# Sparse FFN with routing: every task at a place of its own, sort steps on other operands and engines, DB of two tiles, convolution of three chunks on TensorE

## What is computed

```python
h = _layernorm(x) * (1 + ca) + sa
x = x + ga * _L0_attn_ref(h, ...)      # a state space block
h = _layernorm(x) * (1 + cb) + sb
x = x + gb * _L0_ffn_ref(h, ...)       # a routed FFN
```

## Time and profile before

| | us |
|---|---|
| median of 3 runs | 1594.65 (1587.15 to 1599.17) |
| profiled execution | 1594.51, of which the span is 1592.8 |
| VectorE busy | 1128.7 (71%) |
| TensorE busy | 1211.0 (76%), mean granted clock 0.859 |
| GpSimd busy | 1027.0 (64%) |
| ScalarE busy | 931.1 (58%) |

### The profile page before, as it was taken

How to read it: one execution, slowest core, us unless ns; L and a number is a source line. 1 busy time by engine, 2 the same in 40 slices (tenths; PEclk the granted TensorE clock), 3 DMA queues, 4 the chain that set the end, 5 groups by cost and what they waited for, 6 DMA issues and landing times. The chain is left out here.

```text
span 1592.8 us, 20071 instructions
## 1 busy us (share of the span) xinstructions
PE 1211.0 (76%) x5756; PEld 829.7 (52%) x5756; DVE 1128.7 (71%) x1489; ACT 931.1 (58%) x1772; POOL 1027.0 (64%) x936
## 2 busy tenths in 40 slices
PE   8887677565689898753578898744489999989892
PEld 4566454344456565542356565543356656646461
DVE  5898999998776977885488987995468688601000
ACT  5757775792677567842379667932377647333231
POOL 1676886886775657688895657688874356744222
PEclk9998677586698999966589999966799999999997
DMA  5359635313332322245543233245532335565442
GB/s 189 108 165 281 206 112 170 120 55 114 114 102 78 120 82 99 80 114 175 133 125 100 98 104 100 79 123 181 145 103 80 102 107 160 161 194 143 139 120 72
DMA packets 118929, 201.17 MB, mean 126 GB/s; under 512 B 25876, under 2 KB 34068, under 8 KB 117800
## 3 DMA queue, kind: packets, MB, share of 16 engines
q1 hardware_dynamic: 106536, 166.20, 33.4%
q0 software_dynamic: 12288, 33.69, 8.1%
HBM read 121.97 MB, written 77.88 MB: 125 GB/s over the span
## 5 line engine op out<-in xcount | busy, mean ns | idle before, releaser
L914 POOL TENSOR_TENSOR DB<-DU,BR 128x512 f32<-128x512 f32 x448 | 578.4, 1305 | 174.6 <-DVE H L1351 153.4
L1668 PE MATMUL pb<-ID,H 128*128 128x128 f32 x2048 | 360.2, 313 | 184.6 <-DVE ACC L1376 146.9
L1134 ACT ACTIVATE pb<-DELP,AN 128x512 f32<-128x512 f32 x448 | 306.2, 685 | 273.1 <-DVE H L1351 270.9
L1376 DVE SCALAR_TENSOR_TENSOR ACC<-pb,CTM,ACC 128x512 f32<-128x512 f32 x512 | 373.3, 729 | 105.2 <-PE pb L1668 104.3
L1668 PEld LDWEIGHTS pb<-ID,H 128*128 128x128 f32 x2048 | 278.0, 161 | 279.8 <-DVE ACC L1376 103.1
L1351 DVE TENSOR_TENSOR_SCAN H<-pb,DB 128x512 f32<-128x512 f32 x256 | 310.0, 1211 | 97.6 <-POOL DB L914 78.7
L1351 DVE TENSOR_TENSOR_SCAN H<-pb,ST,DB 128x512 f32<-128x512 f32 x192 | 244.2, 1272 | 14.7 <-ACT pb L1134 14.1
L1221 ACT ACTIVATE YO<-pb,SCO 128x512 f32<-128x512 f32 x106 | 72.3, 682 | 164.4 <-PE pb L1771 129.0
L1490 DVE SCALAR_TENSOR_TENSOR TH<-TH,pb 128x512 f32<-128x512 f32 (+1 forms) x56 | 36.2, 646 | 133.1 <-ACT TH L1203 133.1
L1741 PE MATMUL pb<-WU,XTS 128*128 x424 | 127.2, 425 | 0.0
L1766 PE MATMUL pb<-WD,GT 128*128 x212 | 123.5, 665 | 0.0
(11 more groups left out here) (219 smaller groups left out, 1903.2 us busy)
## 6 DMA issues: line engine op xcount, KB each, us to landing
BR<-bscr SPq DMA_DIRECT2D x112, 256.0 KB, 3.5
XS<-xdr SPq DMA_DIRECT2D x106, 256.0 KB, 3.9
ydr<-YO SPq DMA_DIRECT2D x106, 256.0 KB, 2.7
xdr<-ZX SPq DMA_DIRECT2D x69, 258.0 KB, 4.7
ACC<-in_x SPq DMA_DIRECT2D x16, 512.0 KB, 5.8
DU<-in_x SPq DMA_DIRECT2D x7, 1024.0 KB, 5.8
x1s<-ACC SPq DMA_DIRECT2D x24, 256.0 KB, 3.9
ZX<-x1s SPq DMA_DIRECT2D x24, 256.0 KB, 4.0
```

What stands on the lines that cost most here:

```text
L914: eng.tensor_tensor(DB[:, i % NDB], DU[:, c % 2, r], BR[:, n % 2], ALU.mult).then_inc(S["dbu"], 1)
L1134: eng.activation(DA[i % NDA][:], DEL[:, c % 2, r], ACT.Exp, scale=AN[:, r, n:n + 1]).then_inc(S["da"], 1)
L1376: eng.scalar_tensor_tensor(out=acc, in0=banks[bank_of["flip", c, n, r]][:], scalar=1.0 if n < 0 else CTM[:, c % 2, j, st:st + 1], in1=acc, ...
L1668: t = eng.transpose(b[:, dt * 128:dt * 128 + 128], src[:, dt, r * 128:r * 128 + 128], ID[:])
```

## The change

Nothing is changed in what is computed. GROUPS, the rings DA and H and the banks of `up` and `dn` stay.

- **Places.** The tables by kind are gone. PLACES gives each single task a number of its own, in units of 1/32 slot, and the list is sorted by it; `scan` is at 32 s, `flip` at 32 (s + 6) + 1, `acc` at 32 (s + 6) + 50, `dbu` at 32 s - 93, `da` at 32 s - 30. BANKS gives the bank of each task outright. After the last scan 20 tiles have still to begin; the first tile of group 2 is at slot 422; the gathers of group 0 lie at slots 319 to 363, those of group 1 at 433 to 463 and those of group 2 at 482 to 512.
- **DB of two tiles.** NDB is 6, and in chunks 0 to 6 (but for the first state) one product of 128x1024 makes two tiles: 222 pairs.
- **Convolution on TensorE.** `pe_tiles` is all four channel tiles in chunks 1, 2 and 3 (12 tiles, where there were 2). Diagonal matrices for tiles 0 and 1 are made later (`dg2`), in HT. There are 17 `conv` and 13 pairs `cvs`, `cva` fewer.
- **Sort.** `e0`, `s1`, `e3`, `c3` and a new `sx` are GpSimd's, with 14 instructions for a group; `s3`, `s7` and `c1` are VectorE's, with intermediate values in the PSUM bank of the ranks. The copy `r22` is gone. A token's row carries both scores and its first expert, and `sx` picks the right score after SCO has been loaded; `e4` with its wait for the scatters is gone, and both ways are scattered from the same HT.
- **Smaller things.** NXS is 3 instead of 4 (rows XS in flight). TensorE reads a tile's expert once. JUNK is gone: the squares go to DEL and XN2, with waits on the last user of these and of the small norm tiles.

```diff
-NDA, NDB = 2, 4
+NDA, NDB = 2, 6
-NXS = 4
+NXS = 3
+def pe_tiles(c):
+    return {0, 1, 2, 3} if c in (1, 2, 3) else set()
+def paired(c, n, r):
+    return c not in SPLIT and (c, n) != (0, 0) and r % 2 == 0
...
+    for s in range(W * NC):
+        at += [(32 * s, ("scan", *unit(s))), (32 * (s + LAG) + 1, ("flip", *unit(s))), (32 * (s + LAG) + 50, ("acc", *unit(s)))]
+        if s > 0:
+            at.append((32 * s - 30, ("da", *unit(s))))
+        if s > 1 and not (s % 2 and paired(*unit(s - 1))):
+            at.append((32 * s - 93, ("dbu", *unit(s))))
...
+    left = {what: list(places) for what, places in PLACES.items()}
+    for task in tasks():
+        what = task[0] + "_" if len(task) == 4 and task[2] == -1 else task[0]
+        at.append((left[what].pop(0), task))
+    return head() + [task for _, task in sorted(at, key=lambda x: x[0])]
...
                     if i >= NDB:
-                        eng.wait_ge(S["scan"], i - NDB + 1)
-                    if h is None:
+                        eng.wait_ge(S["scan"], i - NDB + (2 if two else 1))
+                    if two:
+                        eng.tensor_tensor(DB[:, i % NDB:i % NDB + 2], DU[:, c % 2, r:r + 2],
+                                          BR[:, n % 2:n % 2 + 1].to_broadcast([128, 2, CT]), ALU.mult).then_inc(S["dbu"], 2)
+                    elif h is None:
...
+                    eng.tensor_tensor(MK[:, :, 0:n], IO[:, 0:NE].unsqueeze(1).unsqueeze(1).to_broadcast([128, 2, n, NE]),
+                                      IXF[:, :, 0:n].unsqueeze(3).to_broadcast([128, 2, n, NE]), ALU.subtract).then_inc(S["so"], 1)
...
+                    eng.tensor_scalar(tiles, counts, 63.5, 1.0 / 128, ALU.add, ALU.mult).then_inc(S["sd"], 1)
...
-                    eng.wait_ge(S["d_sc"], 16 * (scatters(g) + n))
-                    eng.tensor_tensor(HT[:, 0:n, D], EX[:, 0:n], HT[:, 0:n, D], ALU.mult).then_inc(S["score"], 1)
...
+                    if cs and j == 0:
+                        eng.wait_ge(S["hb"], 2 * cs)
+                        eng.wait_ge(S["g1"], cs)
+                        eng.wait_ge(S["frs"], 3 * cs - 2)
+                    eng.activation(XN2[:, j], acc_tile(cs // 2, 2 * (cs % 2) + j), ACT.Square,
                                    bias=FNG[:, j:j + 1], accum_out=FSQ[:, j:j + 1]).then_inc(S["fsq"], 1)
```

More of the change, by code:

```diff
@@ new lines, in sort, with experts @@
+def sort(g):
+    at = [(what, g) for what in ("e0", "s1", "rk", "e1", "s3", "e3", "s7", "c1", "c3")]
+    at += [("sc", g, way, t) for way in range(2) for t in range(len(tokens(g)))]
+    return at + [("xs", g), ("sx", g)]
+def experts(g):
+    at = []
+    for q in range(n_pairs(g)):
+        at += [(what, g, i) for i in tiles_of(g, q) for what in ("xl", "xt", "xe", "up", "uq")]
+        at += [(what, g, q) for what in ("th", "gg", "gt", "ge")]
+        at += [(what, g, i) for i in tiles_of(g, q) for what in ("dn", "dq", "ye", "yst")]
+    for t, (cs, j) in enumerate(tokens(g)):
+        at += [("gbl", cs // 4)] if cs and cs % 4 == 0 and j == 0 else []
+        at += [("yg", g, t, 0), ("yg", g, t, 1)] + ([("xr", g, t)] if bounced(cs) else [])
+        at += [("zm", g, t), ("fin", g, t), ("out", g, t)]
@@ L361, in schedule @@
-    return order
+    at = []
+    for s in range(W * NC):
[4 more added lines that the diff above has]
+            at.append((32 * s - 93, ("dbu", *unit(s))))
+    for n in range(2, NS * NC):
+        at.append((128 * n - 220, ("br", *divmod(n, NS))))
+    for s in range(W):
+        at.append((32 * s + 19, ("warm", s, WARM["slot"])))
@@ L466, in adaln_kernel @@
             nth[task] = tally[task[0]]
-        at = {task: i for i, task in enumerate(order)}
-        bank_of, freed = {}, {}
-        held, last = {b: None for b in range(2, 8)}, {b: -1 for b in range(2, 8)}
+            for table in (STEPS, STEPS_V):
+                if task[0] in table:
+                    steps[task] = tally[id(table)]
+                    tally[id(table)] += table[task[0]]
+        bank_of, freed, held = {}, {}, {}
+        numbers = {what: list(row) for what, row in BANKS.items()}
         for task in order:
@@ L475, in adaln_kernel @@
             if what in EMPTIED:
-                early = at[EMPTIED[what][0], *k] < at["scan", 1, 0, 0]
-                b = min(range(2, 7) if early else WORK_BANKS, key=lambda b: last[b])
-                bank_of[task], freed[task] = b, held[b]
+                b = int(numbers[what].pop(0))
+                bank_of[task], freed[task] = b, held.get(b)
                 held[b] = (EMPTIED[what][0], *k)
-                last[b] = at[held[b]]
         S = {}
@@ L1494, in _ @@
         def _(eng):
+            expert = {}
             for task in order:
```

626 lines of the change are left out of this document (309 added, 317 removed), and 149 rows, old and new, of tables (PAIRS, PLACES).

## The result

The changed kernel takes 1404.12 us (median of 4 runs, 1402.98 to 1406.19) against 1593.52 for the kernel before beside it (1587.15 to 1599.17). The ratio is 0.8814, with an interval from 0.8778 to 0.8849: 189 us are gone, and 1455 us had been forecast, with a range from 1400 to 1530.

The account below looks back on a forecast made before the run. VectorE idle in stages 0 to 6 (208.5 us), TensorE the bound afterwards; 109 us off slot 422's 1105.2 gives 996, plus 431 for TensorE and 28 of closing chain: 1455 us, own range 1410 to 1480, wide range 1400 to 1530.

Parts of the forecast that it names:

- Taps: Stages 0 to 2: convolution taps of chunks 1 to 3 leave VectorE, saving 3.5, 8.1 and 8.1 us; TensorE's added work hidden.
- The wait for the scatter: Sort's step waiting for a landed scatter goes: 12 us counted in stage 2; in stages 4 and 6 inside the collisions.
- Stage 3: Two tiles fewer and evener places, against 35 us of idle VectorE: 10 us saved.
- Collisions: Stages 4 and 6: gathers on GpSimd move away from another group's scatters, saving 40 and 24 us.
- Rival (a): Gathers still hold up DB in stages 5 and 6, half of the 66 us won comes back: 1488 us; 14%.
- DB pairs: GpSimd: 222 paired products at 2.42 us each; full saving bound 42 us in all, worth nothing where GpSimd has slack.
- From slot 422 to the end: 394 us of TensorE work at the old density of 0.913 is 431 us, plus 28 us of closing chain.
- The second way: Total as 1297 + 7x, x being VectorE's idle time per stage, 0 to 6; 1455 us is x = 22.6.
- (b): After the scans: last group's sum-to-scatter chain starves TensorE, 27 us of idle: 1482 us; 13%.
- (c): Idle time is moved, not removed: x stays 29.8, 1505 us, or 1560 if only taps and sort pay; 6%.
- (d): Every stage: flips stand behind convolution or tile matmuls and VectorE's in-order sums wait; 1619 us at x = 46; 6%.
- (e): Whole kernel: the tables give nothing that can be measured, 1594 us; 3%.

Follow-up runs that it names:

- e8: Changed kernel, with VectorE waiting again in each of the six token groups until all its scatters have landed: 1420.19 us, ratio 0.8913.
- e9: Kernel of e1, with the TensorE products of each pair of expert tiles spread out: 1532.25 us, ratio 0.9635 to the kernel before.
- e1: Kernel before, with only the gathers, products and sums of groups 0 and 1 moved later: 1549.62 us, ratio 0.9719.
- e10: Changed kernel, with the gathers of groups 0 and 1 packed as in the kernel before, a token tile every three slots: 1438.51 us, ratio 0.903.
- e5: Changed kernel, with every product DB made for one tile at a time again, keeping the ring of 6 tiles: 1395.49 us, ratio 0.8768.
- e6: Changed kernel, with each task's PSUM bank chosen by the old rule instead of read from a list: 1409.43 us, ratio 0.8847.
- e2: Kernel before, with the tiles of groups 2 to 5 started denser and earlier, gathers unmoved: 1627.52 us, ratio 1.0205.

## Why the prediction was right, and where it fell short

**Up to slot 422.** The forecast had it at 996 us, and it began at 982.6. Stage by stage, forecast and measured: stage 1 121.6 and 123.9; stage 2 137.9 and 143.0; stage 3 161.1 and 137.8; stage 4 157.2 and 148.1; stage 5 158.1 and 149.2; stage 6 up to slot 422 90.4 and 108.0; stage 0 with its start 170.2 and 172.6. The sum is off by 14 us, and it hides larger errors of opposite sign: stages 3, 4 and 5 came 23, 9 and 9 us below their forecast, stage 6 up to slot 422 18 above, stage 2 5 above.

- *Taps.* Right in kind. Stage 1 lost 5.8 of the 8.1 us counted; stage 0 lost 4.7 with 3.5 counted. TensorE carries the convolutions unseen, as its idle time (26, 43.5 and 55 us) against 47 us of new work had said: the sums of stages 0 to 2 wait for it 0.4, 0 and 7.3 us, no more than before (3.8, 0 and 8.3). A matmul of the convolutions takes 603 and 703 ns against the 591 taken.
- *The wait for the scatter.* Counted, with the rest of the sort, with 12 us in stage 2, "half of that stage's idle time", and with the collisions beyond. That was too much. In stage 2 of the kernel before the wait is 6.5 us (the row below), and the stage's idle time fell by 2.8 us only, from 24.1 to 21.3. VectorE's work fell by 12.2, of which 8 are taps and 4 the sort, so the stage won 15.0 us of 20.1 counted. Putting such a wait back costs 16 us in all, 4.5 in stage 2 (e8). The row of the kernel before, stage 2:

```profile
DVE HT L1422 <- DMA xdr<-HT,POS: 6.5, 1, 6.5
```

- *Stage 3, 10 us counted and 33 measured: the mis-sized term.* "Evener places against 35 us of idle VectorE" had the right mechanism and no price. The row with it was there to be read: in the kernel before 30.1 of the stage's 35 us of idle time are sums that wait for TensorE, which says that tile products stand ahead of them in bunches. Spreading the tiles alone brings 18.5 us (e9). In the kernel after 0.1 us of that wait is left; the two tiles fewer, and an order spread over all tasks, must be the rest, which no run took apart.
- *Collisions.* 40 us counted in stage 4 and 24 in stage 6. 24 slots from 280 take 61.9 us where about 60 were forecast, after 98.7. The gathers' places alone bring them to 71.2 (e1), and the wait for the scatters, put back, costs them 7.6 (e8), which together is nearly all. e1 and e10 give 44 and 34 us for the gathers' places in the whole time, so this, the largest term, stands. Stage 4 got 9 us more than forecast.
- *Stage 5.* Rival (a) priced the gathers' arrival in stages 5 and 6 with half of the 66 us won. In the kernel before it costs 13 us (e1). In the kernel after the stage is 11.9 us shorter than before, no scan of it waits for DB, and all such waits over the whole span are 20.8 us.
- *Stage 6 up to slot 422, 17.6 us more than forecast.* It was counted as if every slot could run at its neighbour's pace. In its 108.0 us VectorE is busy 82.3, and its waits are for the decays (8.0 us), DB (7.9) and smaller ones; TensorE does 92.6 us of work there where the kernel before did 68.7 in the same slots. The waits of this stretch in the kernel after:

```profile
DVE H L1558 <- ACT pb L1342: 8.0, 5, 2.9
DVE H L1558 <- POOL DB L1116: 7.9, 3, 3.6
```
- *DB pairs.* 2398 ns for 2.42 us forecast; in the sum they stood at next to nothing, and e5 shows that this was right: 33 us of GpSimd and not one of the kernel's. Yet the range owes its low end of 1400 to "the full pair saving", which does not exist (and 1410 less 42 would not be 1400 either). Without it the range would have begun at 1410, above the measured time. That 1404 lies inside is luck.

**From slot 422 to the end.** Forecast 431 + 28 = 459 us, measured 392.9 + 28.9 = 421.8. This is the step that failed, 37 us of the 51. It has two factors. *The work*: 394 us forecast, 381.0 measured, worth 13 us. The kernel before needs 400.2 us of TensorE from its slot 422 on, 1742 matmuls; its first 41.7 us ran at a granted clock of 0.61, which my 12 us for ten more slots left out (they held 18.5). The kernel after needs 19.2 us less, for 1717 matmuls. Three rows of this stretch tell the most, two of the kernel before and one of the kernel after:

```profile
L1668 PE MATMUL pb<-ID,H 128*128 128x128 f32 x379 | 59.9, 291 | 16.7 <-DVE ACC L1376 10.2 <-ACT XTS L1195 5.8 <-ACT XH L1169 0.7
L1657 PE MATMUL pb<-DU,DELP 128*128 128x512 f32 x8 | 5.0, 718 | 1.9 <-DVE ACC L1376 1.1 <-ACT XTS L1195 0.8
```

```profile
L1830 PE MATMUL pb<-ID,H 128*128 128x128 f32 x380 | 53.0, 274 | 2.5 <-ACT XTS L1402 2.4
```

The transposes of the scans' results take 274 ns each and not 291, at a mean clock of 0.98 and not 0.93: 6.9 us. The last projections of chunk 7 (these 8 matmuls and 4 smaller ones, 6.3 us) and most of the first tile's front (11 matmuls, 4 us by their mean times) are worked off ahead of slot 422 in the kernel after: some 10 us that are moved and not saved. *The density*: I kept 0.913, and it is 0.970, worth 25 us (394 over 0.913 less 394 over 0.970). I took the old idle time as fixed for this part of the kernel. It was a list of waits; TensorE's from slot 422 on in the kernel before:

```profile
PE pb L1765 <- ACT YO L1221: 18.5, 13, 6.4
PE pb L1724 <- DMA XS<-xdr: 14.3, 2, 13.0
PE pb L1668 <- DVE ACC L1376: 10.8, 5, 6.6
PE pb L1668 <- ACT XTS L1195: 5.8, 3, 4.7
PE pb L1765 <- ACT GT L1211: 4.1, 4, 1.7
```

and in the kernel after:

```profile
PE pb L1927 <- ACT YO L1428: 5.4, 2, 2.9
PE pb L1830 <- ACT XTS L1402: 2.4, 1, 2.4
PE pb L1873 <- POOL MS L1030: 1.8, 1, 1.8
PE pb L1839 <- ACT XH L1364: 1.7, 2, 1.4
```

Behind the first tile, 1146.9 us, the kernel before lost 22.6 of its 36.2 us of idle time to the down products' waits for YO and GT, each a place in an order. It is not the banks that removed them (e6), and spreading the tiles as in e9 does not. What is left of the change is above all the order of all tasks, down products of one tile between the up products of the next; that this is the cause is argued and not shown. The ring of 6 tiles DB, the three rows XS in flight and the sort's moves to GpSimd were not taken apart from it either.

**The second way** shows the error most plainly: 1297 + 7x, where x is VectorE's idle time in each of stages 0 to 6, with x = 22.6. Measured, x is 15.6, so 49 us less. VectorE's work in stages 0 to 6 was 896.8 us for 905 forecast, and stage 7 and the end, 347 us forecast, were 202.4 + 148.9 = 351.3. The forecast itself named 17 as the value with both collisions gone, and then gave 5.6 us a stage back for tiles drawn forward; that was not needed.

**The rivals.** (b) a last group that starves TensorE: the last sum ends at 1263.6 us and the last scatter goes at 1298.1, 34 us apart and not 77, and TensorE is 97% busy across it. (c), (d) and (e) are out by x = 15.6. But (d)'s mechanism is real: e2 brought it about, in stage 7 of the kernel before. By the Trainium skill's rule (SBUF — State Buffer, "Who interferes with whom"), a VectorE operation with two SBUF inputs and a GpSimd one that reads SBUF exclude each other, and each remaining tap could have been held up to 1.2 us longer. Of the 40 taps of the kernel after 9 take 2.2 to 2.5 us, and in e5, with single products, 1 does, while 11 take 1.3 to 1.5. In this sense the trace agrees with the exclusion. But the median of 752 ns stayed, and all taps together take 52.8 us against 50.2 in e5: the doubled DB costs some 3 us, and not 34. Their means, 1319 and 1254 ns at 1152 before, say less, since one tap of 6.3 or 7.6 us is in each; in e10, with pairs and without such a tap, the mean is 1125.

## What to carry to other kernels

Where an engine idles in a stretch in which it is the bound, list its waits there and price each; a density carried over as a factor keeps waits that are only an order. Moving work earlier on a busy engine gains only if it doesn't stand ahead of what another engine's in-order queue needs: the tiles of the last groups drawn closer together cost 34 us, and the products of all tiles spread further apart brought 17. An engine that is overfull in a short stretch only (GpSimd, 94% busy over 85 us in e10 and 69% over its span) is relieved by moving work in time, 34 to 44 us here; making one of its operations cheaper brought nothing that could be measured.

## What was not expected of the hardware

The mean clock granted to TensorE moves with the order of the work, and the time with it: in stage 6, 163.1, 157.6 and 153.8 us for the same 774 matmuls at 0.90, 0.93 and 0.96. A 128x1024 product of GpSimd takes 2398 ns on average, where a single one of 128x512 takes 1311 ns in the same kernel (e5): 9% saved, and none of it reached the end.
